# Layer 0 of a two-layer decoder: the feed-forward joins the attention stream's program, and the output projection runs over two groups of heads

## The reference

```
x = layernorm(x + self_attention(x))         # 16 heads of 16, rotary, causal
x = layernorm(x + gamma * cross(x, ctx))     # 8 heads; keys and values from ctx
x = layernorm(x + ffn(x))

def ffn(x):                                  # hbitlinear, relu squared, hbitlinear
    h = hbitlinear(x, w_up)                  # 256 -> 512
    return hbitlinear(relu(h)**2, w_down)    # 512 -> 256
def hbitlinear(x, w):
    xh = hadamard(x)                         # over the last axis
    scale = 127 / max(abs(xh), per row)
    return (round(xh * scale) / scale) @ ternary(w).T
# self attention: softmax(Q K / 4, causal) V per head; heads side by side; @ Wo
```

## Time and profile before

| | |
|---|---|
| median of 3 timed runs | 877.35 us (875.77 to 881.85) |
| the profiled execution | 880.92 us |
| its span, first to last instruction | 879.1 us |
| busy: PE, DVE, ACT, POOL | 765.6, 613.6, 456.1, 431.9 us |
| mean granted clock of TensorE | 0.92 |

### The profile page before, as it was taken

The page is one execution under the profiler, slowest core; times in us unless marked ns, Lnnn a source line. Parts: engine busy times, 40 slices in busy tenths (PEclk is TensorE's granted clock), DMA queues, the critical chain, the costliest instruction groups (busy, mean ns, idle before and its releaser), DMA issues. The chain is left out here.

```text
span 879.1 us, 18142 instructions
## 1 busy us (share of the span) xinstructions
PE 765.6 (87%) x5770; PEld 481.4 (55%) x5770; DVE 613.6 (70%) x2060; ACT 456.1 (52%) x1447; POOL 431.9 (49%) x427
## 2 busy tenths in 40 slices
PE   6899899987877999999999999999574489999944
PEld 4566666665753444555555555688454445555523
DVE  2656776695694778788888888442355768889856
ACT  2366776573422000688888888300232077777734
POOL 4344654563001666566666666100540368888840
PEclk9869999998986999999999999999795589999976
DMA  9400000000000667500000000160268322222225
GB/s 324 186 1 1 2 2 1 1 2 1 0 1 27 166 161 181 150 1 1 1 1 1 1 2 1 37 270 19 79 242 215 119 62 75 77 75 75 75 73 175
DMA packets 32493, 63.44 MB, mean 72 GB/s; under 512 B 6592, under 2 KB 21324, under 8 KB 31536
## 3 DMA queue, kind: packets, MB, share of 16 engines
q1 hardware_dynamic: 20960, 41.67, 14.8%
q0 software_dynamic: 4896, 11.95, 4.3%
q10 hardware_dynamic: 6544, 8.67, 3.7%
HBM read 41.27 MB, written 9.84 MB: 58 GB/s over the span
## 5 line engine op out<-in xcount | busy, mean ns | idle before, releaser
L1398 ACT ACTIVATE a_room<-a_room,a_nm 128x257 f32<-128x257 f32 x256 | 127.3, 499 | 100.6 <-DVE a_nm L1241 99.8
L1440 POOL TENSOR_TENSOR a_room<-a_room,a_rd 128x1024 f32<-128x1024 f32 x64 | 121.3, 1895 | 65.8 <-DVE a_rd L1249 65.4
L1241 DVE CUSTOM_DVE_ANT_0 a_room<-a_ps,table,NSK 128x256 f32<-128x256 f32 x256 | 107.8, 478 | 0.7 <-PE a_ps L1100 0.4
L584 ACT ACTIVATE l_Pr<-l_Sm,l_nm 128x128 f32<-128x128 f32 (+1 forms) x192 | 88.3, 461 | 36.1 <-DVE l_nm L487 22.0
L613 POOL TENSOR_TENSOR l_Pr<-l_Pr,l_rd 128x256 f32<-128x256 f32 (+1 forms) x80 | 82.0, 1043 | 50.4 <-DVE l_rd L501 50.3
L1100 PEld LDWEIGHTS a_ps<-room 64*128 64x128 f32 x512 | 44.1, 186 | 53.2 <-issue 48.5
L1180 PE MATMUL a_ps<-a_room,W 128*128 128x512 f32 x160 | 72.5, 612 | 0.8 <-ACT a_room L1412 0.8
L1100 PE MATMUL a_ps<-room 64*128 64x256 f32 x512 | 72.3, 402 | 0.5 <-DVE a_nm L1241 0.5
L1221 DVE SCALAR_TENSOR_TENSOR a_room<-a_ps,BQK,table 128x512 f32<-128x512 f32 x80 | 56.4, 746 | 22.9 <-PE a_ps L1180 22.9
L1115 PE MATMUL a_ps<-table,a_room 128*128 128x128 f32 x512 | 69.7, 279 | 1.1 <-ACT a_room L1407 1.1
L1446 POOL TENSOR_TENSOR a_room<-a_room 128x512 f32<-128x512 f32 x20 | 25.4, 1271 | 90.3 <-DVE a_room L1221 90.3
(11 more groups left out here) (312 smaller groups left out, 1778.8 us busy)
## 6 DMA issues: line engine op xcount, KB each, us to landing
room<-a_room SPq DMA_DIRECT2D x96, 64.0 KB, 2.1
room<-a_room ACTq DMA_DIRECT2D x96, 64.0 KB, 2.1
room<-in_w_in SPq DMA_DIRECT2D x1, 6144.0 KB, 17.5
room<-in_c_in SPq DMA_DIRECT2D x1, 4096.0 KB, 13.4
room<-pairs SPq DMA_DIRECT2D x8, 512.0 KB, 8.8
W<-in_w SPq DMA_DIRECT2D x1, 3072.0 KB, 12.8
room<-in_w_out SPq DMA_DIRECT2D x1, 3072.0 KB, 20.4
W<-in_wo SPq DMA_DIRECT2D x1, 2048.0 KB, 8.4
```

Of the source, the lines that this page charges most:

```text
L584: nc.scalar.activation(Pr[:, t % 4, n, 0:n_keys], Sm[:, t % 2, n, 0:n_keys], ACT.Exp, bias=nm[:, t % 2, n:n + 1], scale=-1.0, accum_out=de ...
L1241: nc.vector.tensor_tensor_reduce(out=Sm[:, t % 2, n, 0:S], in0=psS(t)[:, n // 2, n % 2, :], in1=c["window"][:, n % 2, :], scale=-1.0, scal ...
L1398: nc.scalar.activation(Pr[:, t % 4, n, :], Sm[:, t % 2, n, :], ACT.Exp, bias=nm[:, t % 2, n:n + 1], scale=-1.0, accum_out=den[:, t % 2, n: ...
L1440: pool.tensor_tensor(p, p, rd[:, t % 2, :].unsqueeze(2).to_broadcast([P, 4, S]), ALU.mult).then_inc(normed, 1)
```

## The change

1. Two neighbouring self groups of a batch share a unit. `V` gets 48 columns per head, 16 zeros, 16 data, 16 zeros; an even group takes the last 32 of them (data, zeros), an odd one the first 32 (zeros, data). Both accumulate into one bank of `psO`, which then has all 128 rows in use. `AT` has 2 tiles per batch and not 4, `store` runs once per two groups, `WO0` is two tiles without zero rows, and `output` has 2 products per half and not 4. GpSimd clears the zeros of `V` with two strided memsets. Since units and rises of `mixed` now differ, the plan counts `event` beside `unit`.
2. The feed-forward stands in the same `Block` as the stream. Its tiles lie in those of the stream that are dead by then (`QT`, `KT`, `V`, `Pr`, `PT`, `AT`); `psR` is `psS` and `psU` is `psO`, `x_turn` writes to `psR`. On PE, `x_turn(0)` and `x_turn(1)` stand at the end of step 47, `rotate(0)` in step 48 and `rotate(1)` in step 49; behind the stream come `x_turn(2)`, `rotate(2)`, `q_turn(0)`, `up(0)`, `q_turn(1)`, `x_turn(3)`, `rotate(3)`, `up(1)`. ScalarE copies pairs 0 and 1 in steps 48 and 49, and VectorE quantises them at the end of steps 49 and 50. The applies of the last two cross batches stand in steps 50 and 54.

```diff
@@ project_0
-            pool.memset(V[:], 0.0).then_inc(cleared, 1)
+            sides = V.rearrange("p c k (h d) -> p (c k h) d", h=4)
+            pool.memset(sides[:, :, 0:DK0], 0.0)
+            pool.memset(sides[:, :, 2 * DK0:3 * DK0], 0.0).then_inc(cleared, 1)
...
-                out = V.rearrange(...)[:, t // 2, :, t % 2, :, 0:DK0]
+                out = V.rearrange(...)[:, t // 2, :, t % 2, :, DK0:2 * DK0]
@@ Layer0Plan
             self.unit.append(units)
-            units += 1
+            self.event.append(events)
+            units += self.closes(i)
+            events += 1
+
+    def closes(self, i):
+        kind, b, g = self.groups[i]
+        return kind == "cross" or g % 2 == 1
+
+    def opens(self, i):
+        kind, b, g = self.groups[i]
+        return kind == "cross" or g % 2 == 0
@@ layer_0, tensor: mix, output
-                        v, at = V[:, 4 * b + g, kt, rows], kt * P
+                        from_column = n * 3 * DK0 + (DK0 if g % 2 == 0 else 0)
+                        v, at = V[:, 4 * b + g, kt, from_column:from_column + 2 * DK0], kt * P
...
-                                            start=(kt == 0), stop=(kt == 1), skip_group_check=True)
+                                            start=(kt == 0 and plan.opens(i)), stop=(kt == 1 and plan.closes(i)),
+                                            skip_group_check=True)
...
-                    for g in range(4):
+                    for j in range(2):
                         last = nc.tensor.matmul(psO[:, unit % 2, t * D:(t + 1) * D],
-                                                AT[:, 4 * b + g, t * P:(t + 1) * P], WO0[:, g, :],
-                                                start=(g == 0), stop=(g == 3))
+                                                AT[:, 2 * b + j, t * P:(t + 1) * P], WO0[:, j, :],
+                                                start=(j == 0), stop=(j == 1))
                 last.then_inc(s["mixed"], 1)
+
+            def x_turn(p):
+                pe.wait_ge(s["cross_x"], 2 * p + 2)
+                pe.wait_ge(s["maxed"], 4 * (slots - 1 if p < 2 else slots))
+                for i in range(2):
+                    for k in range(KD):
+                        last = nc.tensor.transpose(psR[:, p, (2 * i + k) * P:(2 * i + k + 1) * P],
+                                                   X[:, 2 * p + i, k * P:(k + 1) * P], ident[:, :])
+                last.then_inc(f["xT"], 1)
...
+            def up(p):
+                pe.wait_ge(f["q1Tc"], p + 1)
+                if p == 0:
+                    pe.wait_ge(s["stored"], units)
+                else:
+                    pe.wait_ge(f["hr"], p)
...
@@ layer_0, tensor: the order
                     mix(m)
+                if t == slots - 1:
+                    x_turn(0)
+                    x_turn(1)
+                if slots <= t < slots + 2:
+                    rotate(t - slots)
             x_turn(2)
-            rotate(1)
-            x_turn(3)
             rotate(2)
             q_turn(0)
-            rotate(3)
             up(0)
             q_turn(1)
+            x_turn(3)
+            rotate(3)
             up(1)
             q_turn(2)
@@ layer_0, vector: store, and the order
-                dve.wait_ge(s["mixed"], unit + 1)
+                dve.wait_ge(s["mixed"], plan.event[i] + 1)
                 if kind == "self":
-                    nc.vector.tensor_copy(AT[:, 4 * b + g, :], psO[:, unit % 2, 0:S])
+                    nc.vector.tensor_copy(AT[:, 2 * b + g // 2, :], psO[:, unit % 2, 0:S])
...
-                if 0 <= m < slots and m % 2 == 0:
+                if 0 <= m < slots and m % 2 == 0 and plan.closes(m // 2):
                     store(m // 2)
...
+                if t == slots + 1:
+                    quantise1(0)
+                if t == slots + 2:
+                    quantise1(1)
+            quantise1(2)
@@ layer_0, scalar: the order
+            for t in range(slots + LT):
+                if t < slots:
+                    exps(t)
+                if 0 <= t - LT < slots:
+                    keep(t - LT)
+                if t >= slots:
+                    keep_xt(t - slots)
             nc.scalar.activation(warm[:, 0:1], c["ones"][:, 0:1], ACT.Sqrt)
-            keep_xt(0)
-            keep_xt(1)
             keep_xt(2)
+            keep_q1(0)
+            relu(0)
+            square(0)
+            keep_q1(1)
             keep_xt(3)
+            relu(1)
+            square(1)
@@ decoder, arrays_of
-            WO0 = l0.sb("WO0", [P, 4, D])
+            WO0 = l0.sb("WO0", [P, 2, D])
-                V = a0.sb("V", [P, 4 * B, 2, P])
-                AT = a0.sb("AT", [P, 4 * B, S])
+                V = a0.sb("V", [P, 4 * B, 2, 4 * 3 * DK0])
+                AT = a0.sb("AT", [P, 2 * B, S])
-    wo0 = np.zeros((4, 4, 32, D), np.float32)
-    wo0[:, :, 0:DK0] = g["L0_attn_Wo"].reshape(4, 4, DK0, D)
+    wo0 = g["L0_attn_Wo"].reshape(2, 2, 4, DK0, D).transpose(0, 2, 1, 3, 4)
```

More of the change, by code:

```diff
@@ L338, in __init__ @@
         self.output_at = {}
-        self.unit = []
-        units = 0
+        self.unit, self.event = [], []
+        units, events = 0, 0
         for i, (kind, b, g) in enumerate(self.groups):
@@ new lines, in rotate, with q_turn @@
+            def rotate(p):
+                pe.wait_ge(f["xt"], p + 1)
+                if p == 0:
+                    pe.wait_ge(loads["had"], 16)
+                for i in range(2):
+                    for k in range(KD):
+                        last = nc.tensor.matmul(psR[:, p, i * D:(i + 1) * D], xt[:, p, i, k, :], HAD[:, k, 0:D],
+                                                start=(k == 0), stop=(k == KD - 1))
+                last.then_inc(f["rot"], 1)
+            def q_turn(p):
+                pe.wait_ge(f["q1"], p + 1)
+                if p < 2:
+                    pe.wait_ge(s["copied_a" if p == 0 else "copied_v"], slots)
+                else:
+                    pe.wait_ge(f["q1Tc"], p - 1)
+                for k in range(KD):
+                    for i in range(2):
+                        last = nc.tensor.transpose(psT[:, p % 2, (2 * k + i) * P:(2 * k + i + 1) * P],
+                                                   q1[:, p, i, k * P:(k + 1) * P], ident[:, :])
+                last.then_inc(f["q1T"], 1)
@@ new lines, in up @@
+            def up(p):
+                pe.wait_ge(f["q1Tc"], p + 1)
+                if p == 0:
+                    pe.wait_ge(s["stored"], units)
+                else:
+                    pe.wait_ge(f["hr"], p)
+                for j in range(4):
+                    for k in range(KD):
+                        last = nc.tensor.matmul(psU[:, j // 2, (j % 2) * 2 * P:(j % 2 + 1) * 2 * P],
+                                                TU[:, k, j * P:(j + 1) * P],
+                                                q1T[:, p, k].rearrange("p i t -> p (i t)"),
+                                                start=(k == 0), stop=(k == KD - 1))
+                last.then_inc(f["up"], 1)
@@ new lines, in rotate2 @@
+            def rotate2(t):
+                pe.wait_ge(f["mixed"], t // 2 + 1)
+                if t < 4:
+                    pe.wait_ge(f["q1"], t + 1)
+                else:
+                    pe.wait_ge(f["q2"], t - 3)
+                for a in range(2):
+                    for b in range(2):
+                        last = nc.tensor.matmul(psR[:, t % 4, a * 2 * P:(a + 1) * 2 * P],
+                                                hm[:, t // 2, 2 * a + b, (t % 2) * P:(t % 2 + 1) * P], HAD[:, b, 0:D],
+                                                start=(b == 0), stop=(b == 1))
+                last.then_inc(f["rot2"], 1)
@@ new lines, in q2_turn, with down @@
+            def q2_turn(t):
+                pe.wait_ge(f["q2"], t + 1)
+                if t < 2:
+                    pe.wait_ge(f["q1Tc"], t + 3)
+                else:
+                    pe.wait_ge(f["q2Tc"], t - 1)
+                for k in range(4):
+                    last = nc.tensor.transpose(psT[:, t % 2, k * P:(k + 1) * P], q2[:, t, k * P:(k + 1) * P],
+                                               ident[:, :])
+                last.then_inc(f["q2T"], 1)
+            def down(t):
+                pe.wait_ge(f["q2Tc"], t + 1)
+                if t < 2:
+                    pe.wait_ge(f["hr"], PAIRS)
+                else:
+                    pe.wait_ge(f["taken"], t - 1)
+                for k in range(4):
+                    last = nc.tensor.matmul(psU[:, t % 2, 0:D], q2T[:, t, k, :], TD[:, k, :],
+                                            start=(k == 0), stop=(k == 3))
+                last.then_inc(f["down"], 1)
@@ L473, in _ @@
                     mix(m)
+                if t == slots - 1:
[3 more added lines that the diff above has]
+                    rotate(t - slots)
+            x_turn(2)
+            rotate(2)
+            q_turn(0)
+            up(0)
+            q_turn(1)
+            x_turn(3)
+            rotate(3)
+            up(1)
```

(17 more changed lines are left out.)

421 lines of the change are left out of this document (157 added, 264 removed).

## The result

The changed kernel takes 864.99 us (median of 4 runs, 864.74 to 866.02) where the kernel before took 877.02 beside it: a ratio of 0.985, with a 95% interval of 0.982 to 0.988. That is 12.0 us less. The forecast was 864 (863.8 by its sum), faster. Its profiled execution took 866.02 us with a span of 864.2, 14.9 less than the profiled execution before.

What follows compares the result with a forecast made beforehand. TensorE was taken as the bound in the stream, a chain of TensorE, ScalarE and VectorE after it. 7.2 (output) + 6.4 (early rotations) = 13.6 us off the median 877.35 gave 863.8 us, range 857 to 870.

Steps and rivals of the forecast that it cites:

- Part 1: Output projection over two groups at the four batch ends: 8 records for 16, 1.81 us less each, 7.2 us.
- Parts 2 to 4: Halved AT copies on VectorE, mixes with unchanged count, and V cleared by two strided memsets: each taken as 0.
- the bound of 1.2 us: Clearing V on GpSimd: if 16-element runs cost what the neighbouring add does, the memsets end some 1.2 us late.
- Part 5: First turns and rotations moved under the stream's last slots: second up product about 6.4 us sooner, carried to the feed-forward's end.
- the hand-made order: Predicted start times of TensorE's turns, rotations and up products and VectorE's applies at the end of the stream.
- The one fall of the clock that I counted: A clock fall at TensorE's gap around 220 to 222 us, counted as before; without it 0.7 us more gain.
- in these numbers: The missing block boundary ahead of the feed-forward was taken as already included in the 6.4 us, with no separate gain.
- a change in the length of the later stages: Sign of a wrong forecast: stages after layer 0 differ in length, which nothing in the prediction accounts for.
- B: Rival: clock falls inside the drain at the stream's end, costing 5.3 us, leaving 8.3 in all: 869 us; chance 0.12.
- C: Rival: the output's gain is half hidden behind ScalarE or GpSimd, giving 3.6 us: 867.4 us; chance 0.08.
- E: Rival: TensorE's clock falls at batch boundaries, +0.9 us per slot, up to 899 us; chance 0.04.
- D: Rival: fewer copies ease VectorE behind boundaries (up to 3.3 us), no second clock fall (0.7): 859.8 us; chance 0.08.

Runs made afterwards that it cites:

- changed, again: The changed kernel, nothing altered, run a second time beside the kernel before: 865.7 us, ratio 0.984.
- output only: The kernel before with only the output projection over two groups, the feed-forward staying a program of its own: 885.1 us against 892.9, ratio 0.992.
- filler of products: The kernel before with 8 extra unread matrix products on TensorE behind the stream's last mix, run on two chips: ratios 0.998 and 0.997.
- filler of transposes: The kernel before with 32 unread 128x128 transposes on TensorE behind the stream's last mix: 877.6 us against 879.8, ratio 0.998.
- rotations after: The changed kernel with turns, rotations, copies and quantising of pairs 0 and 1 moved behind the stream's last step: 883.4 us against 892.9, ratio 0.990.
- one program only: The changed kernel with the old output projection, so only the feed-forward in the stream's program: 886.5 us against 892.9, ratio 0.992.

## Why the prediction was right

**What bounds the kernel.** TensorE's line in the stream, and the chain in the drain: a halved output gave its time one to one, and so did VectorE's store once it was out of TensorE's way. In the profiles nothing of layer 0 was lost on the way to the end.

**Part 1, the output: 7.2 forecast, 7.0 measured.** Per batch 1.73 us (3.62 to 1.89), not 1.81. That it adds in full is shown by the run of it alone.

**Parts 2 to 4, taken at 0.** The halved copies gave nothing beyond the output's own time: the distance of the outputs fell by 1.75 us, 1.73 of it the output. The strided memset is 2 x 1.80 us and ends long before 12.8; the bound of 1.2 us, from the 16-element add, was empty: 2048 elements in runs of 16 take what 2048 contiguous ones take, 1.80 us.

**Part 5, the early rotations: 6.4 forecast, 7.1 without a clock fall, 7.2 measured.** Moved onto the new axis (the second-last turn of the stream starts 6.4 us sooner), the hand-made order reads: rotation 0 at 199.9, turn at 201.6, rotation 1 at 203.6, applies at 206.1 and 212.0, rotation 2 at 208.0, up products at 211.0 and 217.1. The trace has 199.88, 201.71, 203.70, 205.96 and 211.75, 208.09, 211.21 and 217.26. From the second-last turn to `up(1)` it is 6.3 us less (25.7, 19.4), against the 6.4 that I carried to the end. The one fall of the clock that I counted did not come in this execution, and what the missing fall gave back is 1.0 us, not my 0.7. It did come in the changed kernel's second profile, and cost 1.5 us there: the tail was 54.7, and part 5 then gives 5.7. So the 6.4 lies between an execution with the fall and one without; which of them comes, nothing in the prediction could tell.

What the prediction did not say is how the 7.2 us divide. The up products tell it, in us from the end of the last norm; from the third of them to the last write of X it is 31.8 to 31.9 us in every profile of this table.

| | first up | third up | falls of the clock ahead of the third |
|---|---|---|---|
| before | 20.2 | 28.6 | at the head; behind the gap ahead of `up(1)` |
| output only | 18.8 | 26.3 | at the head, shorter |
| filler of products (both) | 18.1 | 25.6, 25.5 | none |
| filler of transposes | 19.5 | 28.0 | in the drain; behind the gap ahead of `up(1)` |
| rotations after | 12.9 | 24.4 | behind the gap ahead of `rotate(3)` |
| changed, again | 11.6 | 22.9 | the same |
| changed; one program only | 11.6 | 21.4 | none |

The clock is about 3.0 of it (28.6 to 25.6, two falls). From the first to the third up product the rotations-after kernel needs 11.5 us and the changed kernel, in the same order but without the fall, 9.8: the fall is 1.7. Without it that kernel would stand at 22.7, an estimate. So one program, with the new place of `x_turn(3)` and `rotate(3)` behind `up(0)` that came with it (no run separates the two), is 2.8, and the early rotations are 1.4. I had filed the block boundary under "in these numbers", and its 0.3 us of TensorE's idle said too little of it: it held pair 0 for the last pair's layernorm.

**The sum.** The forecast carried the 13.6 us of two profiled executions over to the median, and the medians differ by 12.0. The difference in the profiles, 14.9, holds 0.6 us lost at the start, where the low-clock stretch ended 1.3 us later (at 60.9 and not at 59.7 us), and 1.2 won in layer 1, where it ended sooner behind the feed-forward. I had named a change in the length of the later stages as a sign of being wrong; neither comes from the change's work. The steps of the sum hold to 0.8 us each. Why the medians differ by 2.2 us less than the 14.2 of the two parts in the profiles is not shown: the interval of the ratio, 10.8 to 15.6 us, holds both, and the old tail, 60.5 in this profile, was 58.1 in another, so the profiled execution before may have had more low clock than the usual one. That 13.6 came so near 12.0 is in part luck.

**The rivals.** B's fall in the drain is real, but not for its reason: it was seen at its place in the filler of transposes, an execution of the old drain, and not in any of the profiles with early rotations. Up to the first up product it cost some 1.5 us there (19.54 against 18.09), not 5.3; the other 1.0 us of that tail is the second fall. C fell with the output alone, E never showed: from 65 to 200 us, over all batch boundaries, the clock kept 1.00 in all profiles. D's part from VectorE's copies was nothing; its other part, the fall that does not come again, is in the changed kernel's first profile and not in its second.

## What to carry to other kernels

A program boundary between two stages holds the first tile of the second for the last tile of the first; here one program, with the order that it allowed, was worth 2.8 us where the boundary showed 0.3 us of idle, even before anything was moved under the stream. Idle of TensorE can cost it its clock too, about 3.0 of the 7.2 us here, but that part differs from one execution to the next, so a tail read from one profile should be split before it is explained. And where the busiest engine waits for a copy, look whether the copy merely stands behind another one in its own queue: the swap of two instructions gave 4.1 us, nearly a third of the change's 13.9 on that chip.

## What the runs showed of the hardware that was not expected

The same idle of 2.10 us in the same instructions was followed by a clock of 1.00 in one execution and of 0.50 in another. The gap of 2.2 to 2.3 us ahead of `rotate(3)` was followed by a fall in two of the five profiles that have it, and so was the gap of 2.25 ahead of the old `up(1)`. The execution with 0.50 behind the 2.10 us took 883.14 us, the longest of its kernel's 11 (median 877.62). On that chip the kernel before spread from 875.4 to 883.2 us in 19 runs, and the filler of products from 874.7 to 878.5 in 10; on the slower chip the filler of products spread as widely as 888.1 to 897.2, so that this is no rule.

A strided memset of GpSimd in runs of 16 elements took 1.80 us for 2048 elements, as much as a contiguous one of the same size (`padded`, in the same profile).

One chip is slower than the others by 13 to 16 us on the kernel before (892.85, and 877 to 880), 11 to 13 of them in layer 1 alone, at about the same mean granted clock (0.927 in the output-only kernel there, 0.926 in the changed kernel here); what of the chip does it is left open.
